# Windowed attention: the band closed by a minimum on VectorE behind the exponential, key tiles in another order, maxima in six of eight steps

## The reference

```
attn = einsum('bqhmd,bkhd->bhmqk', q, k) * sm_scale
mask = (q_pos >= k_pos) & (q_pos < k_pos + SW)          # SW = 64
attn = where(mask, -inf, attn)
w    = softmax(concatenate([attn, sink], -1))[..., :-1]
out  = einsum('bhmqk,bkhd->bqhmd', w, v) @ W_out
```

## Time and profile before

| | us |
|---|---|
| median of 3 runs | 2787.49 |
| runs | 2779.35, 2787.49, 2788.04 |
| the profiled execution, its own time | 2784.71 |
| its span in the trace | 2783.0 |
| TensorE busy | 2524.9 |
| VectorE busy | 1625.8 |
| ScalarE busy | 1262.4 |
| GpSimd busy | 1290.5 |

### The profile page before, as it was taken

The page is one execution under the profiler, slowest core; times in us unless marked ns, Lnnn a source line. Parts: engine busy times, 40 slices in busy tenths (PEclk is TensorE's granted clock), DMA queues, the critical chain, the costliest instruction groups (busy, mean ns, idle before and its releaser), DMA issues. The chain is left out here.

```text
span 2783.0 us, 40695 instructions
## 1 busy us (share of the span) xinstructions
PE 2524.9 (91%) x14471; PEld 1686.0 (61%) x14474; DVE 1625.8 (58%) x2165; ACT 1262.4 (45%) x2175; POOL 1290.5 (46%) x1130
## 2 busy tenths in 40 slices
PE   6887999878999999999878879799999989998798
PEld 5444777654444444444654437578888867775676
DVE  4663555576666766664436533477677745554555
ACT  4464333464555555555334552356555633333222
POOL 4100344485888878888521003345445523442243
PEclk8888999898999999999976889899999988998799
DMA  1000111121101101010000001100000001110111
GB/s 58 1 2 15 40 45 45 44 77 39 39 21 33 39 24 39 17 34 1 27 24 1 1 1 55 47 20 23 29 20 20 24 14 35 45 45 15 30 43 40
DMA packets 39709, 81.63 MB, mean 29 GB/s; under 512 B 7552, under 2 KB 21120, under 8 KB 39040
## 3 DMA queue, kind: packets, MB, share of 16 engines
q1 hardware_dynamic: 39264, 79.41, 10.1%
q10 hardware_dynamic: 288, 0.13, 0.0%
HBM read 59.07 MB, written 2.62 MB: 22 GB/s over the span
## 5 line engine op out<-in xcount | busy, mean ns | idle before, releaser
L2017 DVE TENSOR_REDUCE a1h_mseg<-bank 128x2 f32<-128x1024 f32 x256 | 302.7, 1222 | 187.1 <-PE bank L1774 173.1
L63 POOL TENSOR_TENSOR f_wh<-f_raw,ones_r 128x768 fp32r<-128x768 f32 (+1 forms) x74 | 111.8, 1511 | 541.7 <-PE bank L464 367.0
L1951 ACT ACTIVATE a1h_prob<-bank 128x512 f32<-128x512 f32 x366 | 206.1, 598 | 165.6 <-PE bank L1834 83.8
L1754 POOL TENSOR_TENSOR a_qk<-a_qk,a1h_prob 128x512 f32<-128x512 f32 x186 | 238.6, 1314 | 50.9 <-ACT a1h_prob L1951 50.9
L453 PE MATMUL bank<-x_norm_h,f_wh 128*128 128x512 f32 x592 | 243.9, 412 | 6.4 <-PEq L3186 2.5
L453 PE MATMUL bank<-x_norm_l,f_wh 128*128 128x512 f32 x592 | 238.1, 402 | 0.0
L453 PE MATMUL bank<-x_norm_h,f_wl 128*128 128x512 f32 x592 | 237.9, 402 | 0.0
L656 DVE SCALAR_TENSOR_TENSOR f_tf<-bank,f_bias,f_sg 128x512 f32<-128x512 f32 x148 | 111.1, 751 | 191.4 <-PE bank L453 185.0
L544 ACT ACTIVATE f_hhi<-f_hf 128x512 fp32r<-128x512 f32 x124 | 78.3, 632 | 276.4 <-DVE f_hf L664 276.4
L1832 PE MATMUL bank<-a1h_ql,a1h_k 128*128 128x512 f32 x512 | 203.2, 397 | 0.0
L1847 PE MATMUL bank<-a1h_prob,a_v 128*64 128x512 f32 x732 | 180.0, 604 | 0.0
(11 more groups left out here) (589 smaller groups left out, 6298.1 us busy)
## 6 DMA issues: line engine op xcount, KB each, us to landing
f_raw<-in_l_w_dram SPq DMA_DIRECT2D x66, 385.0 KB, 3.0
a1h_st_q<-a_qk SPq DMA_DIRECT2D x128, 128.0 KB, 2.4
l2a_qkraw<-in_l2a_wqk_dram SPq DMA_DIRECT2D x32, 128.0 KB, 2.2
l2a_vraw<-in_l2a_wvg_dram SPq DMA_DIRECT2D x8, 512.0 KB, 3.8
f_raw<-in_l_w_dram SPq DMA_DIRECT2D x8, 449.0 KB, 3.3
a_qk<-l_keys SPq DMA_DIRECT2D x24, 128.0 KB, 2.6
a1p_raw<-in_l1a_w_dram SPq DMA_DIRECT2D x20, 128.0 KB, 2.1
a_qk<-in_l1a_wo_dram SPq DMA_DIRECT2D x16, 128.0 KB, 2.1
```

What stands on the lines that cost most here:

```text
L63: return pool.tensor_tensor(dst, src, one.to_broadcast(list(src.shape)), ALU.mult)
L1754: pool.tensor_tensor(out, first, slot_of[t % NP], ALU.add).then_inc(sum_done, 1)
L1951: act.activation(slot_of[t % NP], core.bank[2 + t % 3][:, :], ACT.Exp, scale=scale).then_inc(p_ready, 1)
L2017: dve.tensor_reduce(mseg[:, :, qb, s], spare(("A", n, k))[:, :, :], AX.X, ALU.max).then_inc(a_read, 1)
```

## The change

Three things are changed in `attend_window`. The band isn't added to the scores any more: the exponential runs on the open scores, and VectorE then takes the minimum of the slot's part and `open_`, which is 0 in the band and 1e30 elsewhere (`close_bands`, one step behind the exponentials). Who reads a slot with a band waits for `band_closed` too (`wait_weights`). The tiles are taken in an order that spreads those with a band over the steps: tiles 0, 2, 4, 6, 8, 9, 10, 12, 14 have one. The maxima of the next batch, before in steps 0 to 6 by 3, 3, 2, 2, 2, 2, 2, stand in steps 0 to 5 by 2, 1, 3, 4, 4, 2; `row_maxima` moves from step 7 to step 6. The last tile isn't added by GpSimd (26 additions a batch instead of 28), but by two more products of 32 columns in D.

```diff
-    TILES = [(h, kb) for h in range(NH) for kb in range(TB)]
+    TILES = [(0, kb) for kb in (0, 4, 1, 5, 2, 6, 3, 7)] + [(1, kb) for kb in (4, 3, 5, 0, 6, 1, 7, 2)]
...
+    GROUPS = [(0, 1), (2,), (3, 4), (5,), (6, 7), (8, 9), (10, 11), (12, 13), (14, 15)]
...
-        each = (3, 3, 2, 2, 2, 2, 2, 0) if n else (0, 0, 3, 3, 4, 4, 2, 0)
+        each = (1, 1, 2, 2, 2, 1, 0, 0) if n else (0, 0, 2, 2, 3, 2, 0, 0)
...
-            pool.tensor_scalar(mk[:, :, :], mk_raw[:, :, :], 1.0, None, ALU.mult).then_inc(prep, 1)
+            pool.tensor_scalar(open_[:, :], mk_raw[:, 0, 0:BAND], 1e30, None, ALU.add).then_inc(prep, 1)
...
+        def wait_weights(eng, n, i, a):
+
+            eng.wait_ge(p_ready, tile(n, i, a) + 1)
+            if closed(i):
+                eng.wait_ge(band_closed, (n * len(CLOSED) + CLOSED.index(i)) * PER + a + 1)
...
-                    if not kb:
+                    h, p = divmod(i, TB)
+                    if not p or summed_by_tensor(i):
                         continue
...
-                mm = pe.matmul(bank[:, :], k1[:, a, keys], ql[:, n % 2, a, half(h)], start=False, stop=lo >= hi)
-                if lo < hi:
-                    mm = pe.matmul(bank[:, lo - h * HALF:hi - h * HALF], core.ident_b[:, :],
-                                   mk[:, 0, lo - kb * P:hi - kb * P], start=False, stop=True)
-                mm.then_inc(s_ready, 1)
+                pe.matmul(bank[:, :], k1[:, a, keys], ql[:, n % 2, a, half(h)], start=False,
+                          stop=True).then_inc(s_ready, 1)
...
-                        pe.wait_ge(p_ready, t + 1)
+                        wait_weights(pe, n, i, a)
...
+                for a in range(PER):
+                    r = 32 * (2 * a + NH - 1)
+                    wait_weights(pe, n, len(TILES) - 1, a)
+                    mm = pe.matmul(ps[r:r + 32, 0, :], ones, slot_of[tile(n, len(TILES) - 1, a) % NP], start=False,
+                                   stop=True, tile_position=(0, r))
...
+            def close_bands(n, j):
+                for i in (2 * j, 2 * j + 1):
+                    if not closed(i):
+                        continue
+                    h, kb = TILES[i]
+                    lo, hi = band(h, kb)
+                    for a in range(PER):
+                        t = tile(n, i, a)
+                        part = slot_of[t % NP][:, lo - h * HALF:hi - h * HALF]
+                        dve.wait_ge(p_ready, t + 1)
+                        dve.tensor_tensor(part, part, open_[:, lo - kb * P:hi - kb * P], ALU.min).then_inc(band_closed, 1)
...
                     if n + 1 < BATCHES and j == 7:
-                        row_maxima(n + 1)
-                        max_rows(n + 1)
+                        max_rows(n + 1)
+                    if j and n < BATCHES:
+                        close_bands(n, j - 1)
+                    elif not j and n:
+                        close_bands(n - 1, 7)
+                    if n + 1 < BATCHES and j == 6:
+                        row_maxima(n + 1)
```

More of the change, by code:

```diff
@@ L1554, in attend_window, with groups_at, band, closed @@
     MR = (slice(64, P), slice(0, 64))
-    def segments(n, j):
-        each = (3, 3, 2, 2, 2, 2, 2, 0) if n else (0, 0, 3, 3, 4, 4, 2, 0)
-        k0 = sum(each[:j])
-        return range(k0, k0 + each[j])
+    def groups_at(n, j):
+        each = (1, 1, 2, 2, 2, 1, 0, 0) if n else (0, 0, 2, 2, 3, 2, 0, 0)
+        g0 = sum(each[:j])
+        return GROUPS[g0:g0 + each[j]]
+    def band(h, kb):
+        return max(kb * P, h * HALF), min(kb * P + BAND, (h + 1) * HALF)
+    def closed(i):
+        lo, hi = band(*TILES[i])
+        return lo < hi
+    CLOSED = [i for i in range(len(TILES)) if closed(i)]
     order = [("A", 0, k) for g in HEAD for k in g] + [("M", 0)]
@@ L1571, in attend_window @@
                     order.append(("M", n + 1))
-                order += [("A", n + 1, k) for k in segments(n, j)]
+                order += [("A", n + 1, k) for g in groups_at(n, j) for k in g]
             if 0 < n and j in (1, 2, 4):
@@ L1584, in sums, with summed_by_tensor @@
         i, a = divmod(r, PER)
-        h, kb = TILES[i]
-        return n * 28 + h * 14 + ((kb - 1) * PER + a + 1 if kb else a + 1)
+        h, p = divmod(i, TB)
+        return n * 26 + h * 14 + ((p - 1) * PER + a + 1 if p else a + 1)
+    def summed_by_tensor(i):
+        return i == len(TILES) - 1
     with ExitStack() as ctx:
@@ L1740, in _ @@
             for n in range(BATCHES):
-                for i, (h, kb) in enumerate(TILES):
-                    if not kb:
+                for i in range(len(TILES)):
+                    h, p = divmod(i, TB)
+                    if not p or summed_by_tensor(i):
                         continue
@@ L1747, in _ @@
                         out = sum_of[m % 3][:, a, :]
-                        first = slot_of[(t - PER) % NP] if kb == 1 else out
-                        if kb == 1 and m >= 3:
+                        first = slot_of[(t - PER) % NP] if p == 1 else out
+                        if p == 1 and m >= 3:
                             pool.wait_ge(a_ready, use["D", (m - 3) // 2] + 1)
-                        if kb > 1:
+                        if p > 1:
                             pool.wait_ge(sum_done, sums(t - PER))
-                        pool.wait_ge(p_ready, t + 1)
+                        if p == 1:
+                            wait_weights(pool, n, i - 1, a)
+                        wait_weights(pool, n, i, a)
                         pool.tensor_tensor(out, first, slot_of[t % NP], ALU.add).then_inc(sum_done, 1)
@@ L1858, in sums_over_keys @@
                         r = 32 * (2 * a + h)
-                        mm = pe.matmul(ps[r:r + 32, 0, :], ones, sum_of[(2 * n + h) % 3][:, a, :], start=True,
-                                       stop=True, tile_position=(0, r))
+                        pe.matmul(ps[r:r + 32, 0, :], ones, sum_of[(2 * n + h) % 3][:, a, :], start=True,
+                                  stop=h < NH - 1, tile_position=(0, r))
+                for a in range(PER):
[3 more added lines that the diff above has]
+                                   stop=True, tile_position=(0, r))
                 mm.then_inc(a_ready, 1)
@@ L1907, in _ @@
                             max_rows(n + 1)
-                        visit(n + 1, pairs[0:2])
+                        for ks in groups_now[0:1]:
+                            visit(n + 1, ks)
                         if j:
@@ L1912, in _ @@
                             values(n - 1, 7)
-                        visit(n + 1, pairs[2:])
+                        for ks in groups_now[1:]:
+                            visit(n + 1, ks)
                     if n and j == 1:
@@ L1948, in weights @@
                     act.wait_ge(av_done, t - NP + 1)
-                    act.wait_ge(sum_done, sums(t - NP))
+                    was, r = divmod(t - NP, ROWS)
+                    if summed_by_tensor(r // PER):
+                        act.wait_ge(a_ready, use["D", was] + 1)
+                    else:
+                        act.wait_ge(sum_done, sums(t - NP))
                 act.wait_ge(s_ready, t + 1)
@@ L2085, in _ @@
                     if n + 1 < BATCHES:
-                        for k in segments(n, j):
-                            maxima(n + 1, k)
+                        for ks in groups_at(n, j):
+                            for k in ks:
+                                maxima(n + 1, k)
                     if n + 1 < BATCHES and j == 1:
```

13 lines of the change are left out of this document (7 added, 6 removed).

## The result

The changed kernel took 2861.73 us, the median of four runs (2857.53 to 2864.93), against 2787.76 us (2779.35 to 2788.36) for the kernel before. The ratio is 1.0259, with a 95% interval of 1.0240 to 1.0278. The forecast was 2846 us in a range of 2812 to 2890. The profiled execution has a span of 2860.2 us, 77.2 more than the 2783.0 of the kernel before.

What follows compares the result with a forecast made beforehand. TensorE in its program order was taken as the bound. The terms -9 + 47 + 18 + 5 - 12 + 12 = +61 us on the profiled 2784.7 gave 2846 us, in a range of 2812 to 2890.

Steps and rivals of the forecast that it cites:

- 46 to 48: Predicted us between the transposes of successive batches in the second attention, instead of 43.6.
- The bounds as summed: Low and high sums of the terms, +26 (2811) and +91 (2876), beside the forecast's own range 2812 to 2872.
- What TensorE is spared: Per batch 18 mask products go, two fp32 products for the last tile come: net -0.58 us, -9 for 16.
- steps 3 and 4: Four maxima each instead of two; the spreading of inverses waits 1.0 us on reductions: 1.2 a batch, +18 us.
- moved work: Step 0's third maximum moves to step 1, ending a wait in batches with key preparation: -12 us.
- The new wait, step 7: Values behind the row-maximum product wait for tile 12's minima, queued behind `ql` writes: net 3.15 a batch, +47 us.
- The minima's price: VectorE's 18 minima a batch: 351, 287 and 224 ns on 192, 128 and 64 columns, 5.8 us together.
- under 0.45: Sign of rare locks: the 288 minima's mean in us; over 0.8 would mean additions block them.
- The shared reads: GpSimd's additions can block a VectorE minimum, up to 1.25 us each; 0.3 a batch on the path, +5 us.
- minima blocked by additions: Rival, chance 0.20: an addition parts each pair of minima; 3 to 5 us a batch more, 2890 to 2920.
- The clock: TensorE's clock falls behind half of the 15 new gaps, up to 1.8 us each: +12 us, bounds 0 and 27.
- the clock falls at every gap: Rival, chance 0.10: TensorE's clock falls behind every new gap, up to 27 us or a little more: 2860 to 2875.

Runs made afterwards that it cites:

- experiment 3: The changed kernel without the minima on VectorE and the waits for them, so the second attention's mask is left out: 2784.69 us, ratio 1.0001.
- experiment 11: The changed kernel with the maxima spread as before (3, 3, 2, 2, 2, 2, 2 over seven steps) and row maxima back in step 7: 2853.42 us, ratio 1.0235.
- experiment 1: The changed kernel with the minima of tiles 12 and 13 ahead of VectorE's `ql` writes instead of behind them: 2825.9 us, ratio 1.0151.
- experiment 10: The changed kernel with GpSimd's additions cut to 16 columns, so its output isn't the reference's: 2851.22 us, ratio 1.0226.
- experiments 5: experiment 1 plus the last step's bands closed at the end of step 7, ahead of VectorE's work on keys: 2824.37 us, ratio 1.0119.
- experiment 9: experiment 1 plus second-half tiles reordered so step 7's two tiles have no band, and groups of maxima 1, 1, 2, 2, 1, 2: 2804.04 us, ratio 1.0064.
- experiment 12: experiment 9 with GpSimd's additions cut to 16 columns, so its output isn't the reference's: 2780.93 us, ratio 0.9970.
- experiment 2: The changed kernel with ten unread products on TensorE behind the row-maximum product, filling most of the gap: 2855.66 us, ratio 1.0255.

## Why the prediction was right

The time was 15.7 us over the forecast, inside the range, and the mechanism that decides it was the one named. The distances came out at 47.80 where "46 to 48" was written, and their 54.3 us stand against 53, thirteen fifteenths of the forecast's 61. The 15.7 are the first and the last batch, longer than the sum had them, and 5.6 us ahead of the attention, where nothing is changed. The bounds as summed are 2811 and 2876, not quite the range of 2812 to 2872 that stands there; nothing hangs on it. Step by step:

- **What TensorE is spared (-9), steps 3 and 4 (+18), moved work (-12).** Together they were put at -3; experiment 3 measures them together as nothing (ratio 1.0001), and its thirteen distances as -3.3. They hold one by one too: a clean batch goes from 42.83 to 43.43, +0.60 where -9 and +18 over 15 make the same, and the mean of all falls by 0.25 all the same, so the moved work gives 0.85 a batch, 12.8 in 15. R waits 0.91 against a predicted 1.0, D's two products cost 0.86 against 0.93. In experiment 11, with the gap in place and all maxima in their old places, only 3 us of waits for ring buffers came back.
- **The new wait, step 7 (+47).** Right in place, size and number: the values 3.10 later (0.27 to 3.37), and experiment 1, which moves the minima of tile 12 alone, takes 3.0 us out of a batch without keys.
- **The minima's price.** 351 and 287 ns were read from widths; alone they take 346 and 290 (experiment 10). Beside the additions the mean of all 288 is 451 ns, at the edge of the "under 0.45" that stood for rare locks.
- **The shared reads (+5).** The locks on minima are many, 36.6 us, and on the path is about 1.1 at three changes of keys, the lock on the copy of keys included. The rival *minima blocked by additions* didn't happen in this kernel. It stands next behind the gap: in experiments 5 and 9, where the gap is closed, the same locks are on the path, and between experiments 9 and 12 they and the additions' length are worth 23 us.
- **The clock (+12).** Half of the gaps at up to 1.8 were assumed; 12 of 15 lowered it, at 1.4 each: 17 us, of which filling the gap gives back 6. By count that is nearer to the rival *the clock falls at every gap*; by cost it is nearer to the 12 of the sum than to the rival's 27, since each fall cost 1.4 and not 1.8. That two errors met there is luck.
- **What was missing.** The last batch, where GpSimd's additions end late: D waits 3.98 us for them instead of 1.89, and the last two distances are 8.1 longer together; without minima (experiment 3) D waits 0.3. And the first batch, 9.0 longer to its first R. Of these, 6.6 are there in experiment 3 too, so they come from the order of tiles or the places of maxima in the first batch; which of the two wasn't tried.

The 54.3 us of the thirteen distances can be put together from the runs: 13 times 3.0 for the gap (experiment 1), 10 times 1.4 for the clock (experiment 10; three of these thirteen gaps kept it), 3 times 1.1 at the changes of keys, and 13 times -0.25 for all else (43.37 without minima against 43.62) make 53.1.

## What to carry to other kernels

When an engine with a fixed order of instructions has room on average, ask of every instruction added to it what stands ahead of it and when the bounding engine wants its result: some 6 us of VectorE work a batch cost 74 us in these places and 14 in better ones (experiment 9); with short additions beside them the better places took 23 us less again (experiment 12), though no run tells how much of that a kernel without minima would gain too. Closing the worst gap shows the next one, here twice (experiments 1 and 5), so count all the places before promising the gain of one. And look at the spread of starts within a group as well as at the idle time in front of it: a wait shorter than one overlapped matmul is in no view of waits, and such waits were worth 2 us a batch in experiment 9.

## What the runs showed of the hardware

The minima were stretched far more unevenly than one factor could say: 192-wide ones take 346 ns beside short additions (experiment 10) and 396 in the changed kernel, 128-wide ones 290, 745, and 1235 in experiment 11. With GpSimd's additions of 1.3 us cut short both fall to one price, so what differs is which minima meet an addition. The Trainium skill, page "SBUF — State Buffer", section "Who interferes with whom", gives the rule behind it, an exclusive lock for the whole instruction; the trace agrees, with a 16-column row at 1.23 us beside additions (experiment 9) and 0.19 beside short ones (experiment 12).

The clock fell behind 12 of 15 gaps of 2.9 us in the changed kernel and behind all 15 in experiment 10 (0.53 and 0.55 as means of 3.5 and 3 us), and was full again in the window from 3.4 us after the gap's end. It stayed full behind the 5th, 9th and 13th gap, each in the first batch on new keys. With the gap as long but ten products in most of it (experiment 2) it stayed at 1.00. The gaps are alike in length; what makes the difference between batches stayed open.
